# Expert gate through one Silu on ScalarE, upper bound of the up part on VectorE, and a new order of work

## The reference, cut to what matters

```python
h = layernorm(x) * (1 + ca) + sa                    # layer 0, "attention"
x = x + ga * attention16heads(h)                    # scores with a relative term, softmax, values, Wout
h = layernorm(x) * (1 + cb) + sb                    # layer 0, mixture of 16 experts, top 4
gu   = einsum('th,ehf->tef', h, gate_up_proj) + gate_up_bias
gate = minimum(gu[..., ::2], 7.0)
up   = clip(gu[..., 1::2], -7.0, 7.0)
glu  = gate * sigmoid(gate * 1.702)
act  = (up + 1.0) * glu
x = x + gb * einsum('te,teh->th', scores, einsum('tei,eih->teh', act, down_proj) + down_bias)
h = layernorm(x) * (1 + ca1) + sa1                  # layer 1, "memory": phases, sin and cos,
x = x + ga1 * memory(h)                             #   running sums over time, Wo
h = layernorm(x) * (1 + cb1) + sb1                  # layer 1, token mix with relu^2 and a sigmoid
x = x + gb1 * (sigmoid(xr @ W_r) * (relu(xk @ W_k)**2 @ W_v))
```

## Time and profile before

| | us |
|---|---|
| median of 3 runs (lowest, highest) | 1607.24 (1607.21, 1608.69) |
| profiled execution | 1608.18 |
| its span, first to last instruction | 1606.40 |
| one step in the steady part, `x2` to `x2` | 93.5 (504.05 to 597.55) |
| busy: PE, DVE, ACT, POOL | 1407.4, 1215.9, 890.1, 322.2 |

### The profile page before, as it was taken

One profiled execution on the slowest core, in us unless ns is written; L12 is line 12 of the kernel. 1 busy time (PEld: TensorE's weight loads), 2 busy tenths in 40 slices (PEclk: granted clock), 3 DMA queues, 4 the chain that ended last, 5 costly groups with the idle time before them and its releaser, 6 DMA issues.

```text
span 1606.4 us, 24067 instructions
## 1 busy us (share of the span) xinstructions
PE 1407.4 (88%) x7786; PEld 1077.2 (67%) x7786; DVE 1215.9 (76%) x2340; ACT 890.1 (55%) x1446; POOL 322.2 (20%) x261
## 2 busy tenths in 40 slices
PE   3588989999898998989899998989989898999976
PEld 3365766767676676757667675766768576676755
DVE  6747877777787777778777777877778787787665
ACT  1445656565564656556465655646565564656442
POOL 6021221303022130302213030221303022030210
PEclk9979999999999999999999999999999999999898
DMA  7121020303012030301203030120303012030000
GB/s 177 12 25 10 10 28 2 37 1 29 7 12 24 1 36 1 29 8 11 25 1 36 1 29 7 10 26 1 36 1 28 8 10 26 1 33 2 1 4 4
DMA packets 54664, 29.95 MB, mean 19 GB/s; under 512 B 3741, under 2 KB 53610, under 8 KB 54634
## 3 DMA queue, kind: packets, MB, share of 16 engines
q1 hardware_dynamic: 53968, 29.46, 15.8%
q10 hardware_dynamic: 666, 0.11, 0.1%
HBM read 8.20 MB, written 2.10 MB: 6 GB/s over the span
## 4 chain that ended last, share of the span: by engine, by line
issue 41%; PE 39%; DVE 8%; ACT 4%; POOL 3%; DMA 2%; SPq 2%; POOLq 0%; DVEq 0%; ACTq 0%
PE ring L646 13%; PE pb L737 5%; PE pb_v L708 2%; PE ring L633 2%; PE pa L660 2%; PE pb_k L708 2%; SPq L266 2%; DMA k_rows<-qk_part 2%; POOL rstd L349 1%; DVE gsc L1507 1%; DVE prod L1553 1%; PE pb_v L710 1%; PE pb_v L701 1%; PE ring L520 1%; PE pb_k L710 1%
## 5 line engine op out<-in xcount | busy, mean ns | idle before, releaser
L375 POOL TENSOR_TENSOR prob<-gsc,sc_all 128x512 f32<-128x512 f32 x128 | 195.0, 1523 | 263.0 <-DVE gsc L1507 261.6
L646 PE MATMUL ring<-ht,wgu 128*128 128x256 f32 x1024 | 243.4, 386 | 1.6 <-DVE gsc L1507 1.3
L646 PEld LDWEIGHTS ring<-ht,wgu 128*128 128x128 f32 x1024 | 193.5, 193 | 31.3 <-issue 3.4
L1084 ACT ACTIVATE prob<-ring,gub_t 128x256 f32<-128x256 f32 x256 | 106.9, 468 | 136.9 <-PE ring L646 136.0
L1441 DVE TENSOR_REDUCE smax<-ring 128x4 f32<-128x1024 f32 x128 | 153.8, 1220 | 31.4 <-PE ring L544 26.6
L737 PE MATMUL pb<-prod,wo 128*128 128x256 f32 x768 | 175.1, 381 | 0.0
L1507 DVE TENSOR_SCALAR gsc<-ring,gub_t 128x256 f32<-128x256 f32 x256 | 111.7, 477 | 63.3 <-PE ring L646 61.5
L1575 DVE TENSOR_TENSOR_SCAN prod<-keep,prod 128x512 f32<-128x512 f32 x128 | 156.2, 1230 | 0.0
L737 PEld LDWEIGHTS pb<-prod,wo 128*128 128x128 f32 x768 | 143.5, 190 | 18.7 <-DVE prod L1560 0.4
L1034 ACT ACTIVATE prob<-ring 128x1024 f32<-128x1024 f32 x128 | 130.7, 1023 | 28.3 <-PE ring L567 22.8
L660 PE MATMUL pa<-prob,wdown 128*128 128x256 f32 x512 | 129.3, 386 | 3.0 <-DVE prob L1519 3.0
(11 more groups left out here) (268 smaller groups left out, 2745.5 us busy)
## 6 DMA issues: line engine op xcount, KB each, us to landing
q_rows<-qk_part SPq DMA_DIRECT2D x144, 64.0 KB
k_rows<-qk_part SPq DMA_DIRECT2D x144, 64.0 KB
x_in<-in_L_attn_x_dram SPq DMA_DIRECT2D x16, 128.0 KB, 2.1
sc_all<-_L_ffn_gate_up_proj_dram SPq DMA_DIRECT2D x1, 2048.0 KB, 13.3
out_dram<-xo SPq DMA_DIRECT2D x16, 128.0 KB, 1.8
prob<-in_L_wmod_dram SPq DMA_DIRECT2D x2, 384.0 KB, 4.1
wo<-in_L_attn_Wo_dram SPq DMA_DIRECT2D x1, 512.0 KB, 4.3
wk<-in_L_attn_Wk_dram SPq DMA_DIRECT2D x1, 512.0 KB, 5.2
```

The costliest lines, as they stand in the source:

```text
L375: pool.tensor_tensor(gsx[:, n % 2, :], gsc[:, n % NG, :], sca, ALU.mult).then_inc(S["gsc"], 1)
L646: last = mm(ring[:, n % 2, g * 512 + j * L:g * 512 + (j + 1) * L], lhsT=wgu[:, 2 * n + j, g, :], rhs=ht[:, :], start=True, stop=True, skip ...
L1084: af(upc[:, n % NU, j * L:(j + 1) * L], ring[:, n % 2, 512 + j * L:512 + (j + 1) * L], ACT.Relu, bias=gub_t[:, 1, 2 * n + j:2 * n + j + 1] ...
```

## The change

1. The gate moves from VectorE to ACT: `gate_clip` writes Relu(7 - gate) from `ring` to `gsc` (the bias table holds 7 minus the bias), and `bend` makes Silu(1.702 * 7 - 1.702 * that) in place, which is 1.702 * gate * sigmoid(1.702 * gate) of the clipped gate. The factor 1.702 goes out by way of `wdown`, which is scaled by 1/1.702 once.
2. POOL's `expert_pair` multiplies the Silu's result with the scores in place. It now waits for the Silu, and `gsx` is gone.
3. The up part moves from ACT to VectorE: `up` adds bias plus one and takes the minimum with 8; the lower bound is folded in `expert_last` as a maximum with -6. `gated` and `clip_up` are gone.
4. The order of calls is new on all engines, and two waits are written that the order had made needless (`h1` in `head_6`, `h3` in `phase_values`).

```diff
             def expert_pair(b, n):
-                need(pool, "gc", b, 2 * n + 2)
-                need(pool, "gl", b, n - 1)
+                need(pool, "silu", b, n + 1)
                 if n % 2 == 0:
                     need(pool, "bc", b, n // 2 + 1)
                 sca = sc_all[:, 2 * n:2 * n + 2, :].rearrange("p e t -> p (e t)")
-                pool.tensor_tensor(gsx[:, n % 2, :], gsc[:, n % NG, :], sca, ALU.mult).then_inc(S["gsc"], 1)
+                pool.tensor_tensor(gsc[:, n % NG, :], gsc[:, n % NG, :], sca, ALU.mult).then_inc(S["gsc"], 1)
...
-            def up(b, n):
+            def gate_clip(b, n):
                 need(act, "gu_ps", b, n + 1)
-                need(act, "dn", b, n - NU + 1)
+                need(act, "act", b, n - NG + 1)
                 for j in range(2):
-                    af(upc[:, n % NU, j * L:(j + 1) * L], ring[:, n % 2, 512 + j * L:512 + (j + 1) * L], ACT.Relu,
-                       bias=gub_t[:, 1, 2 * n + j:2 * n + j + 1]).then_inc(S["upr"], 1)
+                    af(gsc[:, n % NG, j * L:(j + 1) * L], ring[:, n % 2, j * L:(j + 1) * L], ACT.Relu, scale=-1.0,
+                       bias=gub_t[:, 0, 2 * n + j:2 * n + j + 1]).then_inc(S["gr"], 1)
 
             def bend(b, n):
-                need(act, "gc", b, 2 * n + 2)
-                need(act, "act", b, n - NG + 1)
-                af(th[:, n % NG, :], gsc[:, n % NG, :], ACT.Tanh, scale=0.5 * ALPHA).then_inc(S["th"], 1)
-
-            def clip_up(b, n):
-                need(act, "upr", b, 2 * n + 2)
-                af(upc[:, n % NU, :], upc[:, n % NU, :], ACT.Relu, scale=-1.0, bias=span_up[:, 0:1]).then_inc(S["upc"], 1)
+                need(act, "gr", b, 2 * n + 2)
+                af(gsc[:, n % NG, :], gsc[:, n % NG, :], ACT.Silu, scale=-ALPHA, bias=gate_top[:, 0:1]).then_inc(S["silu"], 1)
...
-            def gate(b, n):
+            def up(b, n):
                 need(dve, "gu_ps", b, n + 1)
-                need(dve, "gl", b, n - NG + 1)
+                need(dve, "dn", b, n - NU + 1)
                 for j in range(2):
-                    ts(gsc[:, n % NG, j * L:(j + 1) * L], ring[:, n % 2, j * L:(j + 1) * L],
-                       gub_t[:, 0, 2 * n + j:2 * n + j + 1], LIMIT, ALU.add, ALU.min).then_inc(S["gc"], 1)
-
-            def gated(b, n):
-                need(dve, "th", b, n + 1)
+                    ts(upc[:, n % NU, j * L:(j + 1) * L], ring[:, n % 2, 512 + j * L:512 + (j + 1) * L],
+                       gub_t[:, 1, 2 * n + j:2 * n + j + 1], LIMIT + 1.0, ALU.add, ALU.min).then_inc(S["upc"], 1)
+
+            def expert_last(b, n):
+                need(dve, "upc", b, 2 * n + 2)
                 need(dve, "gsc", b, n + 1)
-                stt(out=th[:, n % NG, :], in0=th[:, n % NG, :], scalar=1.0, in1=gsx[:, n % 2, :], op0=ALU.add,
-                    op1=ALU.mult).then_inc(S["gl"], 1)
-
-            def expert_last(b, n):
-                need(dve, "upc", b, n + 1)
-                need(dve, "gl", b, n + 1)
-                stt(out=upc[:, n % NU, :], in0=upc[:, n % NU, :], scalar=LIMIT + 1.0, in1=th[:, n % NG, :],
-                    op0=ALU.subtract, op1=ALU.mult).then_inc(S["act"], 1)
+                stt(out=upc[:, n % NU, :], in0=upc[:, n % NU, :], scalar=1.0 - LIMIT, in1=gsc[:, n % NG, :],
+                    op0=ALU.max, op1=ALU.mult).then_inc(S["act"], 1)
```

More of the change, by code:

```diff
@@ L794, in step @@
                 if on_a:
-                    scores(a, 5)
-                    scores(a, 6)
+                    turn_max(a)
+                if on_b:
+                    phases(b, 1)
+                if on_a:
+                    scores_t(a, 0)
+                    scores_t(a, 1)
                 if on_b:
@@ L907, in step @@
                     gate_up(a, 1)
+                    gate_up(a, 2)
+                    gate_up(a, 3)
+                if on_b:
+                    sums_2(b, 3)
+                if on_a:
+                    gate_up(a, 4)
                 if on_b:
@@ L910, in step @@
                 if on_a:
-                    gate_up(a, 2)
+                    gate_up(a, 5)
+                    down_pair(a, 0)
                 if on_b:
@@ L915, in step @@
                 if on_a:
-                    gate_up(a, 3)
+                    down_pair(a, 1)
+                    gate_up(a, 6)
                 if on_b:
@@ L1167, in step @@
                     phase(b, 0)
-                    value(b, 0)
-                    phase(b, 1)
-                    tables(b, 0)
                 if on_a:
```

398 lines of the change are left out of this document (190 added, 208 removed).

## The result

| | before | after |
|---|---|---|
| median (lowest to highest) | 1607.97 (1607.21 to 1612.34), 4 runs | 1635.92 (1631.78 to 1645.98), 4 runs |
| span of the profiled execution | 1606.4 | 1635.2 |
| mean granted clock | 0.953 | 0.896 |

The ratio is 1.0177, 95% interval [1.0127, 1.0227]: slower by 28 us. The forecast was 1619, 12 us slower; the range reached to 1643. The profiled execution of the changed kernel took 1636.89 us, 1.0 above the median of its runs.

A forecast was written before the change was run, and what follows sets the result against it. PE's idle or slow time counted, with VectorE's maxima and ACT's exponentials setting stretches 1 and 2. Stretches of 16.7 + 23.0 + 20.5 + 34.1 = 94.3 against 93.5, over 15 steps 12 us, ends zero: 1619; range 1583 to 1643.

The forecast's parts named there:

- The step: Each of the 15 steps with both parts: 94.3 us against 93.5, 0.8 more, 12 us in all.
- the rival with the low clock: Clock not back before the fourth exponential: stretch 2 grows by 2.5 us more, 1657 us in all; chance 0.12.
- Stretch 1: From `x2` to the first exponential: 16.7 us, 4.1 less than before; bounds 15.7 and 18.5.
- Stretch 2: From the first exponential to `x1`: 23.0 us, 5.9 more than before; bounds 18.5 and 26.
- ACT's list: ACT's work from the first exponential in stretch 2, with tables and two loads: 15.4 us without any wait.
- the clock in this stretch: Low clock in the first 5 us of stretch 2, exponentials 2 and 3 some 0.5 us later.
- the three signs: Signs of wrong: ACT waits for `ring` between exponentials, stretch 4 over 35 us, PEclk 0.50 outside stretch 1.
- The table loads: Seven a step instead of four, two in stretch 2 between exponentials: 1.28 us each, no drain.
- Stretches 3 and 4: Stretch 3, with the second norm: 20.5 us, 1.2 less; stretch 4, with the expert pairs: 34.1 us, 0.2 more.
- The load ahead of `route`'s exponential: Table load claimed to be done before that exponential's input comes, in both orders.
- the new chain Silu, POOL, product: In stretch 4, 0.7 us longer for one pair, costed at nothing because PE is 95% busy there.
- The ends: Step 0 and the last step, some 60 to 80 us each: zero change, plus or minus 5 us.

The follow-up runs named there:

- e5: e4 with the value matmuls of chunks 0 and 1 computing 32 columns of 256: 1632.0 us, ratio 1.0171.
- e3: The changed kernel with Tanh in place of Sin in the tables, two table loads a step instead of seven: 1633.1 us, ratio 1.0149.
- e9: e5 with e3's Tanh in place of Sin, so both ACT's list and the value matmuls are lighter: 1638.9 us, ratio 1.0164.
- e4: The changed kernel with 44 dummy matmuls a step in stretch 1, results unread: 1600.4 us, ratio 0.9950.
- e6: The kernel before with 11 dummy matmuls more a step, behind scores 2, 3 and 4: 1623.9 us, ratio 1.0081.
- e1: The changed kernel's new operations in the old order of calls of the kernel before: 1636.5 us, ratio 1.0173.
- e7: The changed kernel with the old order of calls in step 0 and the last step only: 1621.3 us, ratio 1.0068.
- e11: e7 with e4's dummy matmuls in the 15 middle steps: 1579.4 us, ratio 0.9802.
- e10: The kernel before with 12 dummy matmuls a step, scores 2 and five dummies ahead of the variance: 1585.8 us, ratio 0.9835.

## Why the prediction was right in its direction, and what it had wrong

**The step, 0.8 us longer, was right as a sum, in part by luck.** Forecast 16.7 + 23.0 + 20.5 + 34.1 = 94.3 for a typical step; measured 17.06 + 24.49 + 19.98 + 33.91 = 95.44 where the clock stayed low, and 94.66 as the mean of all 15. The mean agrees because the clock came back early in 5 steps and because errors cancel: stretches 1 and 2 are 0.5 us longer each than forecast (17.16, 23.54), stretch 3 is 0.55 shorter. The total of 1636 lies inside the range only because half of the rival with the low clock had been put into its upper end; that end, 1643, is not the sum that it is said to be (1619 and half of 38 make 1638).

**Stretch 1** went as worked out. After `x2` the maxima that I put at 3.6 started at 3.56 (521.95), the split ended at 12.0 (12.0 forecast) and `copy_max` began at 12.7 (12.7). Only the way from there to the first exponential was 4.4 instead of 3.9: the load ended at 535.04, and then the scores, at the low clock, were 0.4 late.

**Stretch 2** was right in its terms at full clock, and incomplete in its mechanism. ACT's list ran from 159.59 to 174.18 in a step with a high clock, 14.6 for my 15.4, and the stretch was 21.5 for my 22.5. Midway I gave this up for "PE sets the pace", on the sight of PE busy 24.38 of 24.49 us; e5 took 1.8 us of its busy time away and the stretch stayed. But e3 took 2.6 us of loads out of ACT's list and the stretch stayed as well, and with both edits it lost 0.8 (e9). The list was one bound of at least two that end at the same time, and each hides the other.

The term that was mis-sized is the clock in this stretch: 0.5 us forecast, 3.0 to 3.3 measured (24.49 against 21.49 and 21.19). The reason given for it, less work for PE in stretch 1 (busy 13.3 us instead of 16.7), fits e4, where more work there kept the clock. But I let the clock be low only until 5 us into the stretch; it lasted to 544.1, 8.7 us in. Two of the three signs that I had named as "wrong" did appear, ACT waiting for `ring` between exponentials and a clock of 0.50 outside stretch 1. They were the rival "the low clock stays", which had a chance of 0.12, coming true in 10 of 15 steps, on a base 1 us shorter than mine. The Trainium skill (TensorE: Matmul & The Clock Gate, Part 1) says that throttled is the default and activity releases it; e4, e6 and e5 agree, where 44 matmuls more a step kept the clock, 11 behind a wait kept it in only 7 of 15 steps, and less work in stretch 2 lost it.

**The table loads** were rightly priced at 1.28 us each, and no drain was seen behind any of them; the Trainium skill (ScalarE: Activation LUTs, "What ACT_TABLE_LOAD costs") would have had 2.66 a switch. But what they cost the kernel was nothing that can be seen (e3), since ACT then waits for PE as long.

**Stretches 3 and 4** came out 0.5 and 0.2 shorter than forecast. The load ahead of `route`'s exponential, which I had put as done before its input comes, began behind the wait for that input in 13 of its 15 executions (0.74 us of idle time each); the stretch was shorter than forecast all the same, and what this costs was not tried. What I costed at nothing, the new chain Silu, POOL, product, is worth 1.4 us a step in the old order at full clock and 3 with the clock that it loses (e1). The cover that I named was there only because of the new order; I had not worked out what the old one would have shown.

**The ends are the term that failed.** "Zero, plus or minus 5" was put there without following them, and they cost 16.3 us, more than the 15 steps together. Step 0 and the last have only one of the two parts; an order made for a full step leaves its waits open there.

- In step 0, 4.4 of the 9.5 us lie between `x1` and the first `x2`: PE waited 7 us for rows whose release came 5 us later, mostly since ACT's `part` stood behind the broadcast copies (e7).
- The other 5.1 us of step 0 lie ahead of `x1` (86.72 instead of 81.59), all of them behind the first exponential, which started at 64.24, before at 64.81. From there to `x1` the seven kernels with the new order of step 0 took 22.0 to 22.8 us; of the seven with the old one six took 16.8 to 18.3, and e7 took 20.1, where e11, whose step 0 is the same program, took 16.9. So the order costs some 5 us here, up to 3 us can differ between executions of one program, and which wait it is was not followed.
- In the last step PE's waits sum to 23.0 us instead of 18.8, among them those for the phases' products (1.5 to 2.1 us at a time), and the clock was low for 6 us more.

e7 gave some 12 of the 16.3 us back by changing nothing else.

## What to carry to other kernels

Price the first and last iterations of a pipelined loop by themselves: they run the same list with holes in it, and a few waits there outweigh a microsecond a step. Before taking an engine's list for the bound, ask which other chain ends just behind it: here taking out the loads or the value matmuls alone gave nothing, and both together 0.8 us. Where TensorE idles once an iteration, follow its granted clock into the next stretch; in the old order twelve matmuls a step that nobody reads, five of them ahead of the wait behind which the clock fell, were worth 1.7% (e10), and no gain of the reordering over them in the steps is shown.
